# Pairwise attention pooling: transposes and Gram matrices once per four steps, Gram matrices through z's ring

## Chip, cores, metric

The kernel runs on one core of a Trainium2 chip. The metric is the time of one execution in microseconds, as the device measures it, median of several executions.

## What is computed

```python
B, F, D = x.shape                       # 2048, 39, 64; A = 64
row, col = np.triu_indices(F, k=1)      # 741 pairs of fields
ip = x[:, row, :] * x[:, col, :]
hidden = relu(einsum('bpd,da->bpa', ip, W_w) + b_w)
logits = einsum('bpa,a->bp', hidden, W_h) + b_h[0]
a = softmax(logits, axis=1)[:, :, None]
pooled = sum(a * ip, axis=1)
y = pooled @ W_p + b_p                  # [2048, 1], all f32
```

## The kernel before

Pooling and the last product are rearranged: y is the sum over pairs of a times the sum over d of x_i x_j W_p, and that inner sum is an entry of the Gram matrix of one batch, with one operand scaled by W_p. So each batch needs a 39x39 Gram matrix, and of the 741 pairs a hidden layer and a logit. The pairs are stored cyclically: field i with fields i+1 to i+19 (mod 39), so x lies widened to 58 columns (x_wide).

**Sizes.** Two batches share the 128 partitions (a "duo", 64 rows each). A step is 4 duos, 8 batches; there are 256 steps. Sixteen steps are a group, after which softmax and pooling run over 128 batches; 16 groups. Two steps are a "unit" (8 duos).

**One step.** VectorE multiplies 4 duos' pairs into prod (L265, 128x2964). TensorE puts them through the hidden layer in three chunks (hidden_layer, L438): a chunk is 8 matmuls in the code, 64 rows by 32 columns of the array each, 494 columns moved, into one of the two slots of z. ScalarE reads a slot with bias and relu into hidden (rectify, L349). When a step's three chunks are read, two half steps of logits follow on TensorE (first_half, second_half, L458, 8 matmuls each), which add to logits in PSUM. GpSimd places the head's weights for a later step (L226).

**One unit's cross work** (cross_work, L419) has three parts: 8 transposes of a later unit's x (L402), 16 matmuls for the Gram matrices of 8 duos (L413), both into the PSUM tile cross, and behind them VectorE's copies: x into x_wide in two pieces (spread, L250 and L251), the Gram matrices into gram_out (copy_gram, L272). ScalarE scales x by W_p (scale_x, L342), one instruction per unit. SyncE writes gram_out to DRAM, 8 DMAs per unit (L158, L160), and after the last unit of a group loads the values back in banded form, 8 DMAs (L172).

**z's ring.** Chunk n may be written when chunk n-2 has been read: TensorE waits at L432 for hidden_ready, which ScalarE counts up.

**Order.** Every engine's order is written out by hand; there is no scheduler. TensorE's is unit_work (L476). With "F" for a half step of logits and digits for the third of a hidden chunk, one unit is F 1 F 2 F 0 F 1 cross 2 0. Two units are the body of TensorE's inner loop (L518), four bodies a group, and the group loop (L514) holds the opening of logits (L448), which waits until ScalarE's exponentials (L357) have read the logits of the group before. VectorE, ScalarE and SyncE have loops of their own, of two, one and two groups.

```python
def body(k):
    unit_work(AHEAD * k, 0, 2 * k + 1, k + 3)
    unit_work(AHEAD * k + 2, 2, 2 * k + 2, k + 3)
...
with pe.Fori(0, GROUPS - 1) as g:
    pe.wait_ge(logits_free, g + 1)
    open_logits()
    with pe.Fori(0, GROUP_BLOCKS) as w:
        body(GROUP_BLOCKS * g + w)
```

Each f32 matmul of the code is two weight loads and two matmuls in the trace (so a chunk is 16 matmul records), a transpose one of each.

## Time and profile before

| | |
|---|---|
| median of 3 runs | 1133.52 us (1133.19 to 1134.34) |
| the profiled execution | 1133.69 us |
| its span in the trace | 1130.9 us |
| granted TensorE clock, mean over the span | 0.996 |
| TensorE matmuls (PE) busy | 1104.3 us, 98% |
| TensorE weight loads (PEld) busy | 515.5 us, 46% |
| VectorE (DVE) busy | 991.4 us, 88% |
| ScalarE (ACT) busy | 880.9 us, 78% |
| GpSimd (POOL) busy | 304.6 us, 27% |
| DMA | 45.80 MB, 40 GB/s |

The time of an execution holds 2.8 us that lie outside the span. A matmul's end in the trace is modelled and overlaps the next one's start, so start-to-start distances tell more than busy time. The chain of waits goes back from the last instruction, at each step to what released it, and so tells which engine sets the end.

### The profile page before, as it was taken

How to read it: one execution, taken by the hardware profiler on the slowest of the kernel's cores; microseconds unless marked ns; L12 is line 12 of the kernel's file. 1: busy time of each engine (PE TensorE's matmuls, PEld its weight loads, DVE VectorE, ACT ScalarE, POOL GpSimd, SP SyncE). 2: the span in 40 equal slices, each digit the busy share in tenths (PEclk: the TensorE clock that was granted, in tenths of full speed). 3: DMA queues.
4: the chain of work that ended last, by engine and by line, in shares of the span. 5: the costliest groups of instructions: out<-in, count | busy, mean ns of one | idle time of the engine just before them, and what ended most of it. 6: DMA issues, size and time to landing. Idle time of an engine off the chain costs nothing.

```text
span 1130.9 us, 61839 instructions
## 1 busy us (share of the span) xinstructions
PE 1104.3 (98%) x25856; PEld 515.5 (46%) x25856; DVE 991.4 (88%) x741; ACT 880.9 (78%) x929; POOL 304.6 (27%) x263
## 2 busy tenths in 40 slices
PE   6999999999999999999999999999999999999995
PEld 2444444444444444444444444444444444444442
DVE  7989989898898988989889898898989889898891
ACT  3878787787877778787777877877777787877884
POOL 2512214132141412314222141321414114141330
PEclk9999999999999999999999999999999999999998
DMA  2223242321323223132232313213222232321412
GB/s 43 39 43 43 36 47 39 43 40 34 51 38 46 39 36 47 34 52 38 35 50 37 46 34 45 44 34 49 39 37 44 40 46 37 52 36 34 48 25 23
DMA packets 341661, 45.80 MB, mean 40 GB/s; under 512 B 341600, under 2 KB 341600, under 8 KB 341600
## 3 DMA queue, kind: packets, MB, share of 16 engines
q1 hardware_dynamic: 340672, 45.20, 26.8%
q14 instruction: 49, 0.40, 0.2%
q8 instruction: 12, 0.20, 0.1%
q10 hardware_dynamic: 928, 0.00, 0.0%
HBM read 26.59 MB, written 18.54 MB: 40 GB/s over the span
## 4 chain that ended last, share of the span: by engine, by line
PE 95%; ACT 3%; issue 1%; SPq 0%; DVE 0%; DMA 0%; ACTq 0%; DVEq 0%
PE z L438 58%; PE logits L458 29%; PE cross L413 5%; PE cross L402 4%; ACT hidden L349 2%; ACT exps L357 1%; DMA x_rows<-in_r_x_dram 0%; SPq L178 0%; SPq L149 0%; DVE neg_max L278 0%; DVE weighted L287 0%; ACT x_scaled L342 0%; PE logits L448 0%; ACTq L348 0%; DVE x_wide L251 0%
## 5 line engine op out<-in xcount | busy, mean ns | idle before, releaser
L349 ACT ACTIVATE hidden<-z,b_col 128x988 f32<-128x988 f32 x768 | 819.0, 1084 | 224.1 <-PE z L438 223.6
L265 DVE TENSOR_TENSOR prod<-x_wide 128x2964 f32<-128x2964 f32 (+1 forms) x257 | 826.6, 3232 | 37.4 <-PE z L438 37.3
L438 PE MATMUL z<-prod,w_tiles 64*32 64x494 f32 x12288 | 790.4, 580 | 3.3 <-issue 2.2
L226 POOL COPY head_w<-head_cols 128x64 f32<-128x64 f32 x252 | 299.5, 1196 | 794.4 <-PE logits L458 794.4
L458 PE MATMUL logits<-hidden,head_w 64*32 64x371 f32 (+1 forms) x8192 | 437.1, 472 | 4.8 <-ACT hidden L349 3.2
L438 PEld LDWEIGHTS z<-prod,w_tiles 64*32 64x32 f32 x12288 | 236.9, 106 | 238.8 <-issue 117.6
L458 PEld LDWEIGHTS logits<-hidden,head_w 64*32 64x32 f32 x8192 | 180.6, 106 | 239.3 <-issue 234.3
L402 PEld LDWEIGHTS cross<-ident,x_rows 39*128 39x128 f32 x1024 | 42.2, 140 | 109.9 <-issue 109.9
L250 DVE COPY x_wide<-cross 128x312 f32<-128x312 f32 x128 | 61.4, 480 | 32.9 <-PE cross L413 30.4
L342 ACT ACTIVATE x_scaled<-x_wide,wp_col 128x312 f32<-128x312 f32 x128 | 70.2, 549 | 6.2 <-DVE x_wide L251 5.3
L413 PE MATMUL cross<-x_wide,x_scaled 64*39 64x39 f32 x4096 | 65.3, 204 | 0.0
L402 PE MATMUL cross<-ident,x_rows 39*128 39x39 f32 x1024 | 57.0, 236 | 7.2 <-DMA x_rows<-in_r_x_dram 7.2
L272 DVE COPY gram_out<-cross 103x312 f32<-103x312 f32 x128 | 60.4, 472 | 3.9 <-PE cross L413 3.9
L278 DVE TENSOR_REDUCE neg_max<-logits 128x1 f32<-128x742 f32 x16 | 14.9, 930 | 52.1 <-PE logits L458 52.1
L413 PEld LDWEIGHTS cross<-x_wide,x_scaled 64*39 64x39 f32 x4096 | 50.3, 114 | 7.5 <-issue 1.6
L251 DVE COPY x_wide<-cross 128x152 f32<-128x152 f32 x128 | 38.9, 304 | 0.0
L357 ACT ACTIVATE exps<-logits,exp_bias 128x742 f32<-128x742 f32 x16 | 14.0, 872 | 3.6 <-DVE exp_bias L281 3.6
L287 DVE CUSTOM_DVE_ANT_0 weighted<-exps,values 128x742 f32<-128x742 f32 x16 | 14.8, 923 | 1.0 <-ACT exps L357 1.0
L448 PEld LDWEIGHTS logits<-w_tiles 64*32 64x32 f32 x256 | 5.5, 105 | 7.9 <-issue 6.5
L293 DVE TENSOR_SCALAR y_all<-pooled,inv_sum,bp_col 128x1 f32 (+1 forms) x16 | 4.4, 274 | 3.0 <-DVE inv_sum L290 2.7
L342 ACT ACT_TABLE_LOAD x1 | 1.3, 1283 | 7.0 <-issue 7.0
L232 POOL COPY head_w<-head_cols 128x64 f32<-128x64 f32 x4 | 4.3, 1106 | 6.4 <-DMA head_cols<-in_L_rec_W_h_dram 6.4
(15 smaller groups left out, 18.2 us busy)
## 6 DMA issues: line engine op xcount, KB each, us to landing
x_rows<-in_r_x_dram SPq DMA_DIRECT2D x256, 78.0 KB
gram<-gram_out SPq DMA_DIRECT2D x512, 23.8 KB
gram<-gram_out SPq DMA_DIRECT2D x512, 11.6 KB
values<-gram SPq DMA_DIRECT2D x128, 46.3 KB, 3.4
out_dram<-y_all SPq DMA_DIRECT2D x8, 1.0 KB, 2.5
w_tiles<-in_L_rec_W_w_dram SPq DMA_DIRECT2D x4, 16.0 KB, 2.2
head_cols<-in_L_rec_W_h_dram ACTq DMA_DIRECT2D x4, 0.2 KB, 2.4
wp_col<-in_L_rec_W_p_dram ACTq DMA_DIRECT2D x2, 0.2 KB, 2.4
```

Source lines behind the costliest of these rows:

```text
L226: nc.gpsimd.tensor_copy(head_w[:, step % AHEAD, :, :], head_cols[:, :, at:at + TILE]).then_inc(head_w_ready, 1)
L250: nc.vector.tensor_copy(wide[:, :, :, 0:FIELDS], x_cols).then_inc(x_spread, 1)
L251: nc.vector.tensor_copy(wide[:, :, :, FIELDS:WIDE], x_cols[:, :, :, 0:OFFSETS]).then_inc(x_spread, 1)
L265: nc.vector.tensor_tensor(out, one, other, ALU.mult).then_inc(ready, 1)
L272: nc.vector.tensor_copy(gram_out[0:ROWS, slot, :, :, :], cross[0:ROWS, :, GCOLS].rearrange("p j (d f) -> p j d f", f=FIELDS)).then_inc(gra ...
L342: nc.scalar.mul(x_scaled[:, slot, :, :], x_wide[:, slot, :, 0:FIELDS], wp_col[:, 0:1]).then_inc(x_scaled_ready, 1)
L349: nc.scalar.activation(hidden[:, e, :, CHUNK * k:CHUNK * (k + 1)], z[:, (THIRDS * e + k) % 2, :, 0:CHUNK], ACT.Relu, bias=b_col[:, 0:1]).t ...
L357: nc.scalar.activation(exps[:, :, :], logits[:, :, 0:HCOLS], ACT.Exp, bias=exp_bias[:, 0:1], accum_out=exp_sum[:, :]).then_inc(logits_free, 1)
L402: last = nc.tensor.matmul(cross[:, j, FIELDS * q:FIELDS * (q + 1)], duo, ident[rows, :], is_transpose=True, start=True, stop=True, tile_po ...
L413: last = nc.tensor.matmul(cross[col:col + FIELDS, j, GCOLS.start + p * FIELDS:GCOLS.start + (p + 1) * FIELDS], x_scaled[row:row + D, slot, ...
L438: last = nc.tensor.matmul(z[col:col + TILE, (THIRDS * e + k) % 2, b, 0:CHUNK], w_tiles[row:row + D, col:col + TILE], prod[row:row + D, e, ...
L458: last = nc.tensor.matmul(logits[TILE * q:TILE * (q + 1), part, 0:cols], head_w[row:row + A, e, b, :], hidden[row:row + A, e, b, first:fir ...
```

## The change

A block of four steps takes the place of the unit wherever the unit was the grain:

- Cross work once per block: 16 transposes, then the Gram matrices of 16 duos (32 matmuls). Transposes go to x_cols, a PSUM tile of their own. Gram matrices go into a slot of z, as item 6 of a ring of now 13 items per block; ScalarE copies them out (copy_gram, L360 of the new kernel) and counts them in the same semaphore, now z_read.
- VectorE: no copies of Gram matrices; one pair of spreads per block, twice as wide.
- ScalarE: scale_x in four pieces per block, behind chunks 6, 7, 10 and, in the next block, 1; the copy behind chunk 5.
- TensorE's order: per block F 7 F 8 9 F 10 F 11 0 F 1 F 2 3 F 4 F 5 cross 6 (0 to 6 are of the next block). 13 is odd, so the slots swap from block to block; the loop body is now two blocks, run twice per group. The last group is written out without a loop.
- SyncE: half as many DMAs for x and for the Gram matrices, each twice as large.
- At the start the two halves of the first x arrive on semaphores of their own, and ScalarE spreads the second half. At the end half of the 8 stores of y are ScalarE's.

```diff
+    BLOCK_STEPS = 4
+    THIRDS = 3
+    CHUNKS = THIRDS * BLOCK_STEPS
+    ITEMS = CHUNKS + 1
+    CROSS_AT = CHUNKS // 2
+    def item(j):
+        return j + (j >= CROSS_AT)
...
+        def store_y(engine, h):
+            for q in range(QUADS):
...
-            load(0, 0)
+            sp.dma_start(x_rows[0:FIELDS, 0, :, :], x_rows_dram[0, :, 0, :, :]).then_inc(first_x_loaded[0], 16)
             for h in range(2):
                 for c in range(2):
                     sp.dma_start(w_tiles[...], w_hidden).then_inc(w_loaded, 16)
+            sp.dma_start(x_rows[D:D + FIELDS, 0, :, :], x_rows_dram[1, :, 0, :, :]).then_inc(first_x_loaded[1], 16)
             load(1, 1)
...
-                for m in range(GROUP_UNITS):
-                    unit = GROUP_UNITS * g + m
-                    if not (last and m >= GROUP_UNITS - 4):
-                        sp.wait_ge(cross_ready, unit + 3)
-                        load(unit + 4, m % SLOTS)
+                for m in range(GROUP_BLOCKS):
+                    v = GROUP_BLOCKS * g + m
+                    if not (last and m >= GROUP_BLOCKS - 2):
+                        sp.wait_ge(x_cols_ready, v + 2)
+                        load(v + 2, m % SLOTS)
...
+            def block_work(v, slot, pooled_group=None, ended=None, more=True):     # VectorE
+                multiply(v, slot, 0)
+                if pooled_group is not None:
+                    pool_group(*pooled_group)
+                for i in range(1, BLOCK_STEPS):
+                    multiply(v, slot, i)
+                if ended is not None:
+                    find_max(ended)
+                if more:
+                    spread(v + 1, 1 - slot)
...
+            def copy_gram(v, slot, writes):                                        # ScalarE
+                act.wait_ge(z_ready, ITEMS * v + CROSS_AT + 1)
+                if not (isinstance(writes, int) and writes == 0):
+                    act.wait_ge(gram_written[slot], 16 * GRAM_DMAS * writes)
+                nc.scalar.copy(gram_out[0:ROWS, slot, :, :, :],
+                               z[0:ROWS, (slot + CROSS_AT) % 2, :, 0:XCOLS].rearrange("p u (d f) -> p u d f", f=FIELDS)
+                               ).then_inc(z_read, 1)
...
+            def block_work(v, slot, writes, ended=None, more=True):
+                for j in range(CHUNKS):
+                    rectify(v, slot, j)
+                    if j == CROSS_AT - 1:
+                        if ended is not None:
+                            exponentials(ended)
+                        copy_gram(v, slot, writes)
+                    if j == 1 and not (isinstance(v, int) and v == 0):
+                        scale_x(v, slot, 3)
+                    if more and j in (6, 7, 10):
+                        scale_x(v + 1, 1 - slot, (6, 7, 10).index(j))
...
+            def gram_matrices(v, slot):                                            # TensorE
+                pe.wait_ge(x_scaled_ready, BLOCK_STEPS * (v + 1))
+                pe.wait_ge(z_read, ITEMS * v + CROSS_AT - 1)
...
+            def cross_work(v, slot, loads=None):
+                if loads is not None:
+                    pe.wait_ge(x_spread, 2 * (v + 1))
+                    pe.wait_ge(x_loaded[1 - slot], 32 * loads)
+                    transpose(1 - slot, range(2))
+                gram_matrices(v, slot)
...
-                    pe.wait_ge(hidden_ready, THIRDS * step + k - 1)
+                    pe.wait_ge(z_read, ITEMS * v + item(j) - 1)
...
+                first_half(v, 0)
+                chunks(7)
+                second_half(v, 0)
+                chunks(8, 9)
+                first_half(v, 1)
+                chunks(10)
+                second_half(v, 1)
+                chunks(11, 0)
...
+                chunks(5)
+                if following:
+                    cross_work(v + 1, 1 - slot, loads)
+                chunks(6)
+            def two_blocks(n):
+                block_work(2 * n, 0, n + 1)
+                block_work(2 * n + 1, 1, n + 2)
...
-                with pe.Fori(0, GROUP_BLOCKS) as w:
-                    body(GROUP_BLOCKS * g + w)
+                with pe.Fori(0, GROUP_BLOCKS // 2) as w:
+                    two_blocks(GROUP_BLOCKS // 2 * g + w)
...
-            with pe.Fori(BLOCKS - GROUP_BLOCKS, BLOCKS - 2) as k:
-                body(k)
+            two_blocks(BLOCKS // 2 - 2)
+            block_work(BLOCKS - 2, 0)
+            block_work(BLOCKS - 1, 1, following=False)
```

TensorE, the end of the first unit in the loop body of before: a hidden chunk (L438), the waits, the cross work, and the two chunks behind it. ISA and REGISTER_ALU are waits and their arithmetic; x8 counts matmuls as written.

```order
L421 ISA
L396 ISA
L402 MATMUL cross<-ident,x_rows 128x39 x8
L407 REGISTER_ALU
L413 MATMUL cross<-x_wide,x_scaled 39x39 x16
L432 REGISTER_ALU
L438 MATMUL z<-prod,w_tiles 32x494 x8
L430 REGISTER_ALU
L432 ISA
L438 MATMUL z<-prod,w_tiles 32x494 x8
```

The same place in the new kernel, the end of the second block of the loop body and the loop's way back (the two branches are the inner and the group loop's).

```order
L439 MATMUL x_cols<-ident,x_rows 128x39 x16
L444 REGISTER_ALU
L445 REGISTER_ALU
L452 MATMUL z<-x_wide,x_scaled 39x39 x32
L472 REGISTER_ALU
L474 REGISTER_ALU
L481 MATMUL z<-prod,w_tiles 32x494 x8
L567 REGISTER_ALU
L567 COMPARE_AND_BRANCH
L563 REGISTER_ALU
L563 COMPARE_AND_BRANCH
L491 MATMUL logits<-w_tiles 32x2 x8
```

Both counts doubled, the phase comes half as often, the Gram matrices wait for z's ring (L445), and one chunk instead of two stands behind them. The other pairs of adjacent chunks stand elsewhere; this is the one of chunks 8 and 9 (0 to 11 within a block) in the new order, ahead of a half step of logits (L501).

```order
L481 MATMUL z<-prod,w_tiles 32x494 x8
L472 REGISTER_ALU
L474 REGISTER_ALU
L481 MATMUL z<-prod,w_tiles 32x494 x8
L509 REGISTER_ALU
L510 REGISTER_ALU
L501 MATMUL logits<-hidden,head_w 32x370
```

Before there is one such pair per unit, two in four steps, and both stand behind cross work. Now there are three per block (8 9, 11 0, 2 3), none of them behind cross work.

ScalarE, one block of the new kernel (the third of the program); before, a unit was six of L349 and one x_scaled of 128x312.

```order
L356 ACTIVATE hidden<-z,b_col 128x2x494 x4
L365 COPY gram_out<-z 103x624
L356 ACTIVATE hidden<-z,b_col 128x2x494
L340 ACTIVATE x_scaled<-x_wide,wp_col 128x156
L356 ACTIVATE hidden<-z,b_col 128x2x494
L340 ACTIVATE x_scaled<-x_wide,wp_col 128x156
L356 ACTIVATE hidden<-z,b_col 128x2x494 x3
L340 ACTIVATE x_scaled<-x_wide,wp_col 128x156
```

The copy came from VectorE, and the scaling is cut in four.

## Rows read from the trace of the kernel before

**Rows 1.** Page: busy time by engine; the chain that ended last, by engine.
```profile
PE 1104.3 (98%) x25856; PEld 515.5 (46%) x25856; DVE 991.4 (88%) x741; ACT 880.9 (78%) x929; POOL 304.6 (27%) x263
...
PE 95%; ACT 3%; issue 1%; SPq 0%; DVE 0%; DMA 0%; ACTq 0%; DVEq 0%
```

**Rows 2.** Chain of waits, one unit from 521.84: start, us, what, records.
```profile
521.84 0.37 PE cross L402 x8
522.21 0.44 PE cross L413 x32
522.65 1.82 PE z L438 x32
524.47 0.62 PE logits L458 x16
525.09 0.95 PE z L438 x16
...
526.66 0.83 PE z L438 x16
...
530.39 0.37 PE cross L402 x8
```

**Rows 3.** Timeline of TensorE's weight loads, then matmuls, cross work at 530: start, us.
```profile
530.32 0.33 PEld L402 LDWEIGHTS cross<-ident,x_rows 39*128 39x128 f32 x8 [0.81 <-issue]
530.70 0.39 PEld L413 LDWEIGHTS cross<-x_wide,x_scaled 64*39 64x39 f32 x32
...
531.13 1.89 PE L438 MATMUL z<-prod,w_tiles 64*32 64x494 f32 x32
...
533.53 1.04 PE L438 MATMUL z<-prod,w_tiles 64*32 64x494 f32 x13
```

**Rows 4.** Windows: an ordinary unit, then one across a group's end.
```profile
521.77:530.32 8.55, 8.55 (x207) 3.99 (x200) 8.55 (x6) 6.76 (x7) 6.01 (x3) 1.00 0.23 39
...
504.17:513.22 9.05, 8.76 (x223) 4.38 (x217) 8.82 (x11) 7.52 (x9) 0.87 (x2) 1.00 0.22 38
```

**Rows 5.** Groups by line: busy us, mean ns, idle before, releaser.
```profile
L349 ACT ACTIVATE hidden<-z,b_col 128x988 f32<-128x988 f32 x768 | 819.0, 1084 | 224.1 <-PE z L438 223.6 <-issue 0.3
...
L342 ACT ACTIVATE x_scaled<-x_wide,wp_col 128x312 f32<-128x312 f32 x128 | 70.2, 549 | 6.2 <-DVE x_wide L251 5.3 <-DMA bp_col<-in_L_rec_b_p_dram 1.0
...
L272 DVE COPY gram_out<-cross 103x312 f32<-103x312 f32 x128 | 60.4, 472 | 3.9 <-PE cross L413 3.9
```

**Rows 6.** TensorE's timeline, start of the program.
```profile
14.12 3.55 PE L438 MATMUL z<-prod,w_tiles 64*32 64x494 f32 x32 [2.18 <-issue]
...
21.50 1.99 PE L438 MATMUL z<-prod,w_tiles 64*32 64x494 f32 x32 [1.08 <-ACT hidden L349]
...
24.78 0.55 PE L458 MATMUL logits<-hidden,head_w 64*32 64x371 f32 x8 [0.28 <-ACT hidden L349]
```

**Rows 7.** Timeline of SyncE's queue, end of the program.
```profile
1114.37 4.14 SPq L172 DMA_DIRECT2D values<-gram  x8
...
1123.30 3.76 SPq L208 DMA_DIRECT2D out_dram<-y_all  x8
```

**Rows 8.** DMA queues that carry instructions, in 0:45, 45:1055 and 1055:1131.
```profile
q8 instruction: 5, 0.08, 0.7%
...
q14 instruction: 47, 0.39, 0.2%
...
q8 instruction: 7, 0.11, 0.6%
```

**Rows 9.** Timeline of SyncE's queue: middle of its loop body, then its way back.
```profile
356.67 4.43 SPq L172 DMA_DIRECT2D values<-gram  x8
361.37 1.45 SPq L149 DMA_DIRECT2D x_rows<-in_r_x_dram  x2
...
425.70 4.51 SPq L172 DMA_DIRECT2D values<-gram  x8
434.54 0.85 SPq L149 DMA_DIRECT2D x_rows<-in_r_x_dram  x2
```

More of the change, by code:

```diff
@@ L299, in unit_work @@
                     find_max(ended)
-                multiply(2 * unit, unit, slot, 0)
-                if not (isinstance(unit, int) and unit + 1 >= UNITS):
-                    spread(unit + 1, 1 - slot)
-                copy_gram(unit - 1, 1 - slot, earlier)
-                if ended is not None:
-                    pool_group(ended, parity, loads)
-                multiply(2 * unit + 1, unit, slot, 1)
-            spread(0, 0)
-            multiply(0, 0, 0, 0, slice(0, QUADS, 2), first_prod_ready)
@@ new lines, in _ @@
+            spread(0, 0, first=True)
+            multiply(0, 0, 0, slice(0, QUADS, 2), first_prod_ready)
+            multiply(0, 0, 0, slice(1, QUADS, 2))
+            for i in range(1, BLOCK_STEPS):
+                multiply(0, 0, i)
+            spread(1, 1)
+            group(0)
+            with dve.Fori(0, (GROUPS - 2) // 2) as k:
+                group(2 * k + 1, (2 * k, 0, k + 1))
+                group(2 * k + 2, (2 * k + 1, 1, k + 1))
+            block_work(BLOCKS - 3, 1, pooled_group=(GROUPS - 2, 0, GROUPS // 2))
@@ L390, in _ @@
+            for m in range(GROUP_BLOCKS):
+                v = BLOCKS - GROUP_BLOCKS + m
+                block_work(v, m % SLOTS, v // 2, ended=GROUPS - 2 if m == 0 else None, more=m < GROUP_BLOCKS - 1)
             exponentials(GROUPS - 1)
+            act.wait_ge(y_ready, GROUPS)
+            store_y(act, 1)
         @block.tensor
         def _(pe):
-            def transpose(slot, loads):
-                pe.wait_ge(x_loaded[slot], 32 * loads)
-                nc.tensor.sem_inc(z_claimed, 1)
-                for q in range(QUADS):
-                    for j in range(2):
-                        rows = slice(j * D, j * D + FIELDS)
-                        duo = x_rows[rows, slot, 2 * q:2 * q + 2, :].rearrange("f h d -> f (h d)")
-                        last = nc.tensor.matmul(cross[:, j, FIELDS * q:FIELDS * (q + 1)], duo, ident[rows, :],
-                                                is_transpose=True, start=True, stop=True, tile_position=(j * D, 0))
-                return last
@@ L419, in cross_work, with transpose @@
-            def cross_work(m, slot, loads, with_x=True):
-                pe.wait_ge(gram_copied, m + 1)
-                if with_x:
-                    transpose(slot, loads)
-                gram_matrices(m + 1, slot).then_inc(cross_ready, 1)
-            def hidden_layer(step, e, k):
-                if isinstance(step, int) and step == 0:
+            def transpose(slot, tiles):
+                for d in range(ROW_DUOS):
+                    for u in tiles:
+                        rows = slice(u * D, u * D + FIELDS)
+                        duo = x_rows[rows, slot, 2 * d:2 * d + 2, :].rearrange("f h d -> f (h d)")
+                        last = nc.tensor.matmul(x_cols[:, u, FIELDS * d:FIELDS * (d + 1)], duo, ident[rows, :],
+                                                is_transpose=True, start=True, stop=True, tile_position=(u * D, 0))
+                last.then_inc(x_cols_ready, 1)
```

337 lines of the change are left out of this document (156 added, 181 removed).

## The prediction

> **What bounds the kernel now.** I read the page's busy times and chain first: the chain is TensorE for 95%, ScalarE for 3% [rows 1]. So time is won or lost where TensorE's order has something else than full chunks and logits. The chain over one unit [rows 2] shows this as a sum. A chunk is 0.83 us, a half step of logits 0.62, and a unit has six and four of them: 7.46 us. The unit takes 8.55 [rows 2, 4]. The other 1.09 us are 0.37 of transposes, 0.44 of Gram matrices, 0.16 in the two chunks behind them (1.82 in place of 1.66), and 0.12 in a chunk that takes 0.95. The last one is a wait on z's ring: the first chunk behind the cross work starts at 531.13, and the chunk that reuses its slot at 533.53 [rows 3], 2.40 us later, while two chunks and a half step (2.28) lie between. ScalarE idles 224 us waiting for z, and its relu takes 1084 ns [rows 5]: it is not full, it is the latency of the ring that counts. 128 such units are nearly the whole span; a unit across a group's end takes 0.50 more, 9.05 [rows 4].
>
> **The cross phase.** Per four steps before: 2 x (0.37 + 0.44 + 0.16) = 1.94 us. Afterwards there are 16 transposes and 64 matmul records of Gram matrices in one phase. What one more transpose or matmul costs is read from the weight loads [rows 3]: 8 loads of transposes fit in 0.33 us, of which the last one alone is about 0.14 (42.2 us over 1024 on the page), so three steps from pair to pair take 0.19, 0.06 each; 32 loads of Gram matrices fit in 0.39, the last about 0.11, so seven steps from four to four take 0.28, 0.04 each. The larger phase costs 0.37 + 4 x 0.06 = 0.61 and 0.44 + 8 x 0.04 = 0.76, and 0.16 at the edge once: 1.53. That saves 0.41 per block. Bounds: if nothing of the two phases is fixed except the edge, only 0.16 is saved; 0.45 if more of 0.37 is fixed.
>
> [...] The row shows 24 written matmuls in 0.81 us, 34 ns each [rows 2]. [...]
>
> **The ring.** The 2.40 us are the same for every pair of adjacent chunks. Before there are two pairs per four steps, 0.12 each, 0.24. Now there are three (8 9, 11 0, 2 3), and in each 2.28 us of work stand against 2.40. A chunk that starts late also loses what its second half restarts with, some 0.03. I take 0.14 each, 0.42, and 0.03 more between chunks 5 and 6, which have only the phase between them. That gives back 0.21 per block (bounds 0.12 and 0.30). The Gram matrices as a ring item do not wait: item 4's slot was read long before, and the copy of 103x624 must end before chunk 7, 0.76 + 0.83 + 0.62 us after the Gram matrices start. For its price the nearest rows are relu and scaling: 1084 ns for 988 elements, 549 for 312 [rows 5], so about 0.8 for 624. Chunk 7 needs the end of the Gram matrices (0.8), 0.1, 0.8 and 0.15 = 1.85, below 2.21. The copy costs nothing, with 0.3 us of cover.
>
> **ScalarE and VectorE.** ScalarE gets 64 copies (51 us), and its scalings go from 549 ns each to four of about 0.42 per block, 0.6 more per block. That makes 881 + 51 + 37 = 969 us, 87%. Scalings stand where the next chunk is a chunk plus a half step away (1.45 us): relu 0.98 in sequence and 0.33 fit. VectorE loses 60.4 us of Gram copies [rows 5] and some 20 us of spreads, down to some 910. The transposes now also wait for the spread of the block before, and logits for nothing new; the spread starts a phase's end after its transposes and lasts 1.3 us, a whole block before it is asked for. VectorE's four products (3.2 us each) follow the spread and are each needed at least 3 us after they end.
>
> **Group ends.** Before, the logits opened there wait for a relu that stands behind the exponentials. Now exponentials stand behind chunk 5, chunk 6 runs beside them, and the first half step needs no late relu: 0.50 becomes about 0.3. 15 ends, 3 us.
>
> **Start.** The first half step of logits starts at 24.78 [rows 6], with the same work done ahead of it before and now. Before, TensorE stands still 2.18 and 1.08 us there [rows 6] because ScalarE scales the second unit, which waits behind VectorE's products, before its first relu. That order is gone. I take 4 us; bounds 2 and 6.
>
> **End.** The 8 stores of y take 3.76 us to issue on one queue [rows 7], 1.9 on two. Against that the last values: the last Gram matrices come 9.5 us ahead of TensorE's end, in DMAs twice as large, and their 8 loads take 4.14 us to issue [rows 7]. Up to 2 us of wait are possible. I take 1 us of gain.
>
> **Sum.** 62 blocks of steady work x (0.41 - 0.21) = 12.4, group ends 3, start 4, end 1: 20.4 us. The span goes from 1130.9 to 1110.5. The profiled execution is 1133.69, 0.2 above the median of 1133.52; so 1133.7 - 20.4 = 1113. With the bounds (0.16 to 0.45, 0.12 to 0.30 per block) this case by itself is 1104 to 1124.
>
> **Rivals.**
>
> *TensorE's program falls out of its instruction memory at each group's way back.* This is the case on the other side, slower. Queue q8 brings TensorE's program in pieces of 16 KB: 5 pieces in the first 45 us, none between 45 and 1055 while the loops run, 7 when the last group is entered and left [rows 8]. By then the first lap was through about 440 + 850 entries, so a piece is about 256 entries, and at least six pieces are held at a time (the group loop lies in pieces 1 to 5, counted from 0, and the next is fetched ahead). Entries of the loop: 96 written f32 matmuls per unit with 4, 8 transposes with 2, are 400; the body of before is 800 and some 50 for waits. The new body is 1600 and some 90. It starts near entry 440, as before, and ends near 2170: pieces 1 to 8, and 9 is fetched ahead. It stays only if nine pieces fit. What a miss costs, SyncE's rows show: its loop body is left at the end of L172, 430.21, and goes on at 434.54, 4.3 us later, against 0.27 in the middle of the same body, 361.10 to 361.37 [rows 9], with instruction pieces on q14 [rows 8]. TensorE has a chunk queued then, 0.83, and the exponentials to wait for, so 3.0 to 4.1 us are lost per group, 14 times: 42 to 57 us. TensorE idle that long may also fall to the lower clock; two chunks take 3.55 us at the low level and 1.99 at the high one [rows 6], so up to 1.6 us or more each time. 1113 + 50 + 11 = 1174, range 1155 to 1200. If eight pieces or fewer are held, this decides. For it: SyncE's rows. Against it: no row shows TensorE's capacity, and its loops of before never miss.
>
> [...]
>
> *The phase saves only its edge.* If matmuls of 39 columns do not run closer in a long phase, the saving is 0.16 per block and the ring takes 0.21 back: 1133.7 + 3 - 8 = 1129, still faster by start and ends, and within 0.2% (2.3 us, about what a measurement of this kernel can tell from none) only if these fail too.
>
> *ScalarE becomes late.* If its copy from PSUM takes 1.2 us instead of 0.8 or the scalings 0.55, chunk 7 or 9 starts 0.1 to 0.3 late in each block: 1113 + 62 x 0.2 = 1125.
>
> **Chances.** Forecast, with ScalarE on time: 0.45, at 1113. ScalarE late 0.06, phase not dearer than its edge 0.05, both faster or the same. Instruction memory 0.42. Other slips 0.02. Faster by over 0.2% 0.54, within 0.03, slower 0.43. [...] The range must reach into the slower case: 1105 to 1190 holds nearly all of the faster cases and about two thirds of the slower one. The forecast's own range is 1104 to 1124.
>
> **What would show it.** Right: transposes of a block 16.85 to 16.95 us apart (17.10 now), 0.95 or so in one chunk of each of three pairs, cross phase 0.6 and 0.75, VectorE at 910 us, q8 silent between the first groups and the last. Wrong by the rival: q8 with pieces in every group, some hundred instead of 12, a hole of 3 to 4 us in TensorE every 68 us behind chunk 6, and a mean granted clock below 0.99. Wrong by ScalarE: waits of chunk 7 on gram_out L365.

## The result and the profile after

The changed kernel takes 1333.66 us (median of 4 runs, 1328.53 to 1338.32) against 1133.89 for the kernel before beside it: ratio 1.176, interval [1.172, 1.181]. That is slower by 200 us, on the other side of the forecast (1113) and beyond the range (1105 to 1190). The profiled execution took 1334.73 us, with a span of 1332.9.

The page of the changed kernel (busy times, granted clock over the span, instruction queues, the chain of waits by engine, groups of section 5):

```profile
PE 1156.1 (87%) x25856; PEld 517.9 (39%) x25856; DVE 934.6 (70%) x484; ACT 951.3 (71%) x1123; POOL 286.6 (22%) x263
...
PEclk9998989999899998989989899898998989989998
...
q8 instruction: 145, 2.38, 0.8%
...
q14 instruction: 11, 0.09, 0.0%
...
PE 85%; issue 12%; ACT 1%; DMA 1%; SPq 1%; ACTq 0%; DVE 0%; DVEq 0%
...
L491 PE MATMUL logits<-w_tiles 64*32 64x2 f32 x256 | 8.3, 185 | 96.3 <-issue 96.3
```

The number of matmuls is the same as before, the chain has 12% of "issue" in place of 1% [rows 1], and 96 us of idle time stand in front of the opening of the logits (L491), which happens 16 times. q8, which brings TensorE's program, moved 145 pieces in place of 12. It moved them all through the loops, 104 of them in the stretch 100:1045, where before there was none [rows 8]. The same stretch of the changed kernel, DMA queues:

```profile
q8 instruction: 104, 1.70, 0.8%
```

Where the time goes is read from TensorE's timeline over one way back of the group loop:

```profile
93.40 0.82 PE L452 MATMUL z<-x_wide,x_scaled 64*39 64x39 f32 x64
94.24 1.06 PE L481 MATMUL z<-prod,w_tiles 64*32 64x494 f32 x16
98.74 0.24 PE L491 MATMUL logits<-w_tiles 64*32 64x2 f32 x8 [3.44 <-issue]
102.57 0.28 PE L491 MATMUL logits<-w_tiles 64*32 64x2 f32 x8 [3.58 <-issue]
103.11 1.49 PE L501 MATMUL logits<-hidden,head_w 64*32 64x371 f32 x16 [0.26 <-issue]
104.32 1.93 PE L481 MATMUL z<-prod,w_tiles 64*32 64x494 f32 x16
...
109.41 1.06 PE L481 MATMUL z<-prod,w_tiles 64*32 64x494 f32 x16
...
120.30 0.56 PE L452 MATMUL z<-x_wide,x_scaled 64*39 64x39 f32 x34
122.18 0.50 PE L452 MATMUL z<-x_wide,x_scaled 64*39 64x39 f32 x30 [1.32 <-issue]
122.61 1.06 PE L481 MATMUL z<-prod,w_tiles 64*32 64x494 f32 x16
...
132.79 0.84 PE L501 MATMUL logits<-hidden,head_w 64*32 64x370 f32 x6
135.48 0.53 PE L501 MATMUL logits<-hidden,head_w 64*32 64x371 f32 x5 [1.86 <-issue]
...
137.39 0.47 PE L501 MATMUL logits<-hidden,head_w 64*32 64x370 f32 x1
```

Two holes stand next to each other, the second in the middle of sixteen equal little matmuls. No wait for data stands between them, so it is the program itself that is late: the branch back (L563) takes 3.85 us here, 3.4 to 4.0 at each of the 14 way backs, and q8 starts pieces at 95.6 and 99.9 us. The edge between two pieces lies there, eight matmuls into the opening; the trace has some 20 instructions of the loop ahead of it, so its first piece holds little more. Counted in the trace's instructions (a written f32 matmul is four), the two later holes lie 767 and 1279 behind this one, which is three and five pieces of 256. In e2_pad16 below, which puts 16 entries ahead of the loop, all three edges come 15 or 16 instructions earlier in the loop, and the pair of holes shows as one of 6.47 us ahead of the opening. Behind the first two holes a chunk ends 1.93 us after its start, in place of 1.06. The windows of the same group (length, busy us and count of PE, PEld, DVE, ACT, POOL, then granted clock, DMA share, GB/s), whole, its first lap, its second lap, and the stretch of the holes:

```profile
98.60:180.70 82.10, 71.52 (x1616) 32.22 (x1616) 58.54 (x31) 59.32 (x70) 18.24 (x16) 0.96 0.29 38
98.60:140.00 41.40, 34.24 (x708) 15.68 (x716) 24.37 (x13) 25.51 (x30) 5.08 (x7) 0.92 0.19 31
140.00:180.70 40.70, 37.28 (x920) 16.54 (x904) 34.17 (x18) 33.81 (x41) 13.16 (x9) 1.00 0.40 44
99.90:106.80 6.90, 3.98 (x56) 1.67 (x63) 2.80 (x1) 0.43 (x1) 0.00 (x0) 0.51 0.43 67
```

The granted clock is at its lower level, 0.51 over the last of these windows, for the 6.8 us from 100.0. TensorE had then been idle for 3.4 us, had done eight small matmuls and was in the second hole. A group takes 82.1 us. A group of the same code without holes takes 68.2 (shown below), so 13.9 are lost. From start to start: 3.64 in the first hole (chunk to opening 4.50 against 0.86), 3.76 in the second (opening to half step 4.37 against 0.61), 1.84 at the low clock (103.11 to 109.41 against 4.46), 1.54 in the first hole of the first lap (120.30 to 122.61 against 0.77), 2.19 in the second (half step to half step with two chunks between, 132.79 to 137.39, against 2.41). These are 13.0 of the 13.9. The second lap has no hole: its starts from transposes to transposes are 17.0 and 16.87 us.

### The profile page after: what moved, and what is told of

Read it like the earlier page. It is cut to its first block, busy times and chain, and to the rows that moved or that the text cites. A ratio compares the mean times of both kernels' runs of the same rounds, so it can differ in the third digit from the quotient of the medians.

```text
span 1332.9 us, 60251 instructions
## 1 busy us (share of the span) xinstructions
PE 1156.1 (87%) x25856; PEld 517.9 (39%) x25856; DVE 934.6 (70%) x484; ACT 951.3 (71%) x1123; POOL 286.6 (22%) x263
## 4 chain that ended last, share of the span: by engine, by line
PE 85%; issue 12%; ACT 1%; DMA 1%; SPq 1%; ACTq 0%; DVE 0%; DVEq 0%
PE z L481 52%; PE logits L501 25%; PE z L452 4%; PE x_cols L439 3%; ACT hidden L356 1%; PE logits L491 1%; DMA values<-gram 0%; DMA gram<-gram_out 0%; DMA bp_col<-in_L_rec_b_p_dram 0%; SPq L188 0%; ACTq L398 0%; SPq L176 0%; SPq L174 0%; ACTq L392 0%; ACTq L393 0%
## 5 line engine op out<-in xcount | busy, mean ns | idle before, releaser
L481 PE MATMUL z<-prod,w_tiles 64*32 64x494 f32 x12288 | 833.9, 590 | 4.6 <-ACT hidden L356 2.8
L501 PE MATMUL logits<-hidden,head_w 64*32 64x371 f32 (+1 forms) x8192 | 489.6, 491 | 33.9 <-issue 33.4
L501 PEld LDWEIGHTS logits<-hidden,head_w 64*32 64x32 f32 x8192 | 197.7, 109 | 279.3 <-issue 271.8
L259 DVE COPY x_wide<-x_cols 128x624 f32<-128x624 f32 (+1 forms) x64 | 51.4, 804 | 246.1 <-PE x_cols L439 244.1
L340 ACT ACTIVATE x_scaled<-x_wide,wp_col 128x156 f32<-128x156 f32 x256 | 105.9, 414 | 1.2 <-DMA bp_col<-in_L_rec_b_p_dram 1.2
L491 PE MATMUL logits<-w_tiles 64*32 64x2 f32 x256 | 8.3, 185 | 96.3 <-issue 96.3
L452 PE MATMUL z<-x_wide,x_scaled 64*39 64x39 f32 x4096 | 56.5, 202 | 20.6 <-issue 20.6
L365 ACT COPY gram_out<-z 103x624 f32<-103x624 f32 x64 | 43.4, 678 | 37.6 <-PE z L452 37.6
L439 PEld LDWEIGHTS x_cols<-ident,x_rows 39*128 39x128 f32 x1024 | 38.0, 139 | 57.5 <-issue 54.9
L452 PEld LDWEIGHTS z<-x_wide,x_scaled 64*39 64x39 f32 x4096 | 47.0, 113 | 26.3 <-issue 23.4
L439 PE MATMUL x_cols<-ident,x_rows 39*128 39x39 f32 x1024 | 45.6, 233 | 6.5 <-DMA x_rows<-in_r_x_dram 6.5
L491 PEld LDWEIGHTS logits<-w_tiles 64*32 64x32 f32 x256 | 6.2, 121 | 110.6 <-issue 110.6
L260 DVE COPY x_wide<-x_cols 128x304 f32<-128x304 f32 (+1 forms) x64 | 29.5, 461 | 0.0
```

The source lines that it names most:

```text
L259: nc.vector.tensor_copy(wide[:, :, :, 0:FIELDS], cols).then_inc(x_spread, 1)
L260: nc.vector.tensor_copy(wide[:, :, :, FIELDS:WIDE], cols[:, :, :, 0:OFFSETS]).then_inc(x_spread, 1)
L340: nc.scalar.mul(x_scaled[:, duos, :], x_wide[:, slot, duos, 0:FIELDS], wp_col[:, 0:1]).then_inc(x_scaled_ready, 1)
L365: nc.scalar.copy(gram_out[0:ROWS, slot, :, :, :], z[0:ROWS, (slot + CROSS_AT) % 2, :, 0:XCOLS].rearrange("p u (d f) -> p u d f", f=FIELDS) ...
L439: last = nc.tensor.matmul(x_cols[:, u, FIELDS * d:FIELDS * (d + 1)], duo, ident[rows, :], is_transpose=True, start=True, stop=True, tile_p ...
L452: last = nc.tensor.matmul(z[col:col + FIELDS, at, u, FIELDS * d:FIELDS * (d + 1)], x_scaled[row:row + D, duo, :], x_wide[row:row + D, slot ...
```

## The experiments

The table gives what the traces show of each: pieces on q8, start of the first opening of the logits, the first group, the mean of the 14 groups behind it, the time from the last opening to the end of TensorE's last matmul, and the time measured. e2, e3, e4 and e8 were executed once each; their differences are far larger than the spread of any kernel here.

| kernel | q8 | opening | group 1 | groups 2-15 | last | us |
|---|---|---|---|---|---|---|
| before | 12 | 24.2 | 68.9 | 68.9 | 61.5 | 1133.5 |
| changed | 145 | 19.2 | 79.5 | 82.1 | 70.4 | 1333.7 |
| e1_pad64 | 19 | 29.5 | 73.6 | 68.9 | 68.7 | 1151.1 |
| e2_pad16 | 145 | 21.5 | 84.1 | 82.1 | 68.5 | 1340.2 |
| e3_pad128 | 73 | 38.5 | 71.2 | 72.4 | 70.9 | 1211.2 |
| e4_before_two | 142 | 23.5 | 72.6 | 77.4 | 61.4 | 1254.2 |
| e5_fit | 19 | 19.3 | 74.3 | 69.2 | 70.3 | 1146.3 |
| e6_fit_load_first | 19 | 19.4 | 71.9 | 68.3 | 70.6 | 1134.0 |
| e7_slot | 19 | 21.2 | 73.2 | 68.3 | 67.2 | 1134.1 |
| e8_hint | 19 | 19.2 | 78.8 | 69.5 | 74.0 | 1161.4 |
| e9_short_tail | 12 | 21.0 | 73.7 | 68.5 | 65.6 | 1136.6 |
| e10_hint_load_first | 19 | 19.3 | 74.5 | 68.5 | 74.4 | 1143.1 |
| e11_slot48 | 19 | 21.8 | 69.0 | 68.3 | 67.5 | 1128.7 |
| e12_slot48_only | 20 | 21.1 | 71.1 | 68.5 | 67.4 | 1134.9 |

### Which pieces the loop lies in

**e1_pad64**, the changed kernel with this ahead of TensorE's group loop:

```
+            for _ in range(64):
+                nc.tensor.sem_inc(spare, 1)
             with pe.Fori(0, GROUPS - 1) as g:
```

> Edit: 64 semaphore increments that nobody waits for stand ahead of TensorE's group loop in the changed kernel; the loop and its work are untouched. They push the loop's first entry from about 477 to 541, so that it lies in pieces 2 to 8 of 256 entries instead of 1 to 8. Theory (eight pieces are held, the one fetched ahead included, so the loop must lie in seven): q8 falls silent between the first and the last group (some 15 pieces in all instead of 145), no hole at the way back, blocks 16.9 us apart throughout, granted clock 1.0, and the time is the 1113 us that was forecast for the other terms (1104 to 1124), plus at most 2 us for the 64 entries. Rival A (fewer than eight pieces are held, so seven pieces and one ahead do not fit either): 1300 to 1335 us, pieces in every group. Rival B (the hole at the way back is a wait of the new order, for example on logits_free behind the exponentials, and the pieces only follow it): nothing changes, 1333 us.

Measured 1151.12 us, ratio 1.015 [1.013, 1.018]. q8 brought 8 pieces up to 69 us, none until 1068, then 11. The page:

```profile
span 1150.6 us, 60315 instructions
...
q8 instruction: 19, 0.31, 0.1%
```

126 of the 145 pieces and 182 us go with 64 entries that do nothing. Rivals A and B fall: seven pieces and one ahead fit, and the order of the work is the same. But the time is 38 us above what the theory added to it, 1113; the sections below look for them.

**e2_pad16** is the same edit with 16 entries, **e3_pad128** with 128.

> Edit: 16 such entries instead of 64. The loop begins at about 493, still in piece 1, and ends in piece 8. Theory (pieces of 256 entries, eight held with the one ahead): nothing is gained, 1325 to 1340 us and about 145 pieces on q8, which shows that it is the edge between pieces that counts and not the entries or the later start. Rival A: also 1333. Rival B: 1333. Rival C (what counts is the size of the loop against some start offset, or the padding itself helps by delaying TensorE): a time between 1113 and 1333.

> Edit: 128 such entries. The loop begins at about 605 in piece 2 and ends at about 2336, in piece 9: again eight pieces and one ahead. Theory: slow again, 1300 to 1340 us, some 130 to 145 pieces on q8. Rival (only the number of the first piece matters, or a pad of any size above 35 helps): 1113 us as with 64.

e2_pad16 took 1340.18 us with 145 pieces, as expected: what counts is whether the loop's first entry lies behind the edge. e3_pad128 took 1211.18, with 73 pieces, between the two. Six of its way backs bring nine pieces, the others none; the two groups with none at either end take 68.3 and 68.6 us, the others 71.5 to 74.2. The loop reaches only some 40 entries into its eighth piece. The reading is that the piece behind it is asked for just before the branch and comes only at some way backs: q8 starts one at 178.2 us with the branch that starts at 178.1 and takes 4.60 us, and none at those that take 0.21. The theory gave the direction; its 1300 was wrong because it took that for certain.

**e4_before_two**, the kernel before with its body twice:

```
-                with pe.Fori(0, GROUP_BLOCKS) as w:
-                    body(GROUP_BLOCKS * g + w)
+                with pe.Fori(0, GROUP_BLOCKS // 2) as w:
+                    body(GROUP_BLOCKS * g + 2 * w)
+                    body(GROUP_BLOCKS * g + 2 * w + 1)
```

> Edit: the kernel before, with the body of TensorE's inner loop written out twice and half as many laps. Order, waits and work of every engine are as before; the loop is 1690 entries long, from about 480 to 2205. Theory: it becomes slow like the changed kernel, 1133 + 200 = 1333 us (1310 to 1350), with pieces in every group and the clock down once per group. Rival B (the new order causes the holes): 1133 us, q8 silent in the middle.

1254.15 us with 142 pieces. Nothing of the change is in it, and it loses 121 us. TensorE's timeline has the same pair of holes in the opening:

```profile
96.11 0.28 PE L448 MATMUL logits<-w_tiles 64*32 64x2 f32 x7 [3.31 <-issue]
98.97 0.29 PE L448 MATMUL logits<-w_tiles 64*32 64x2 f32 x9 [2.58 <-issue]
```

The size was missed by 80 us: 8.5 per group, not 14. The two later holes of the first lap are absent here. The first of them lies inside the Gram matrices, where two phases of the kernel before have become one and entries pass fastest. The other lies in an ordinary half step: its piece starts on q8 at 132.8 us, only as TensorE reaches its edge (the half step starts at 132.79), while the others behind the opening, in the lap of that timeline, start some 100 to 140 entries ahead of theirs. Why that one is fetched so late stays open.

### A hint in place of a shift

**e8_hint**, the changed kernel with

```
-            with pe.Fori(0, GROUPS - 1) as g:
+            with nc.Fori(0, GROUPS - 1, engines=[mybir.EngineType.PE], hint_back_edge=True) as g:
```

> Edit: the changed kernel as it was (loop in pieces 1 to 8, load of x behind the Gram writes), but each lap of the group loop begins with a hint that names its way back, so that the first piece can be fetched before the branch is taken. Theory (nine pieces for eight places: every piece of the loop has gone when it is wanted, and is fetched one ahead afterwards): the hint takes away the first hole of a group, 3.4 to 4.0 us, and perhaps the low clock behind it; the second hole and the nine pieces per group stay: 14 x 4 to 14 x 8 less than 1333, 1220 to 1280 us. Rival A (the hole at the way back is all that costs, since later pieces are fetched in time): about 1150, like the version that fits. Rival B (the hint finds no room, because the piece is pushed out again before the branch): 1333.

1161.38 us: near rival A, but for a reason that none of the three had. The loop stayed in pieces 1 to 8, and not one piece was fetched between 57 and 1071 us. The page:

```profile
q8 instruction: 19, 0.31, 0.1%
```

TensorE's timeline at the same way back:

```profile
97.03 1.06 PE L481 MATMUL z<-prod,w_tiles 64*32 64x494 f32 x16
98.03 0.44 PE L491 MATMUL logits<-w_tiles 64*32 64x2 f32 x16
98.76 0.86 PE L501 MATMUL logits<-hidden,head_w 64*32 64x371 f32 x16 [0.29 <-issue]
```

The opening follows the chunk after 1.00 us. The trace has an instruction BRANCH_PREFETCH_HINT at L563 in each of the 15 laps, 15 instructions more than the changed kernel in all, and the branch back takes 0.23 us, where the changed kernel's takes 3.83 (medians). That a piece is fetched on the hint is not shown: none came in the laps. Before the loops settle, q8 brings seven pieces here, the last at 56.7 us, and eight in e1_pad64, the last at 68.4. So eight pieces are held, and without the hint one of the eight places goes to the next piece in order, which the loop never needs. With it the loop may fill all eight. This and e1_pad64 settle the capacity: seven pieces and the one ahead fit (e1, e5 to e7), eight and the one ahead do not (changed, e2, e4), eight alone do (e8, e10).

### What was missing to the forecast

**e5_fit** puts the shift where TensorE has nothing to do:

```
             pe.wait_ge(ident_ready, 3)
+            for _ in range(12):
+                nc.tensor.matmul(x_cols[0:FIELDS, 1, BANK - 4:BANK - 2], ident[0:FIELDS, :], ident[0:FIELDS, 0:2],
+                                 start=True, stop=True, tile_position=(0, 0))
             pe.wait_ge(first_x_loaded[0], 16)
```

> Edit: the changed kernel with 12 small matmuls (48 entries, into columns of x_cols' bank that nobody reads) that TensorE does while it waits for the first x rows, in place of the 64 semaphore increments ahead of the loop. The group loop again begins in piece 2 (about entry 524) and ends in piece 8 (about 2256). Those 64 increments took TensorE from 19.5 to 29.5 us, 0.15 us each, and the clock fell behind them. Theory (it is only the piece of the first entry that counts): q8 silent from about 70 to 1060 us, the first opening of the logits at 19 to 21 us as in the changed kernel (29.5 with the increments), the first group 72 to 74 us, later groups 68.2 to 69.2 us as with the increments: 1138 to 1143 us. Rival (the 10 us hole came from the first lap's pieces, which come 5 to 9 us apart, and not from the increments): 1148 to 1152. The forecast's 1113 would need the 7 us in the last group, the 1 us per group in the middle and the first lap's 5 us to be gone too: not expected.

1146.31 us, 1.011 [1.010, 1.013]. The opening is at 19.3 as expected: the 64 increments had cost 10 us, about 0.14 us each (29.5 against 38.5 us with 64 more). Time and first group are above their ranges by some 3 us and a little.

**e6_fit_load_first** changes SyncE's order as well. What led to it are two views of e1_pad64. TensorE's chunk 11 is the first half of the first row, and ends by 487.4; ScalarE's relu of it is the last row, and starts 0.8 us later:

```profile
486.36 2.00 PE L482 MATMUL z<-prod,w_tiles 64*32 64x494 f32 x32
```

ScalarE, same stretch:

```profile
486.07 1.08 ACT L357 ACTIVATE hidden<-z,b_col 128x988 f32<-128x988 f32 x1 [0.33 <-PE z L482]
487.06 0.41 ACT L341 ACTIVATE x_scaled<-x_wide,wp_col 128x156 f32<-128x156 f32 x1
488.23 2.06 ACT L357 ACTIVATE hidden<-z,b_col 128x988 f32<-128x988 f32 x2 [0.76 <-PE z L482]
```

The view names z, but z was complete; x was being loaded at that time. The edit:

```
-                    if not (last and m >= GROUP_BLOCKS - 2):
-                        sp.wait_ge(x_cols_ready, v + 2)
-                        load(v + 2, m % SLOTS)
+                    if not (last and m >= GROUP_BLOCKS - 3):
+                        sp.wait_ge(x_cols_ready, v + 3)
+                        load(v + 3, (m + 1) % SLOTS)
```

with load(2, 0) behind a wait ahead of the first group.

> Edit: as e5_fit, and SyncE issues the load of x for block v + 3 as soon as the transposes of a phase are done, ahead of the eight writes of Gram matrices instead of behind them. In the run with 64 increments ScalarE's relu of chunk 11 began 0.2 to 0.8 us late in 21 blocks (7.9 us in all), with 389 to 699 packets of x in the 1.3 us before it; in the 15 blocks where no x load ran there it was never late. Theory (the traffic of the x load over that relu delays it): with the load 4 us earlier, relu 11 is no longer late; if the same traffic delays any relu, others (chunks 5 to 8) are late instead, with some of it hidden: between 0 and 9 us faster than e5_fit. Rival (the lateness belongs to chunk 11's place, behind the scaling of chunk 10, and the load has nothing to do with it): within 1 us of e5_fit and relu 11 late as often. A third: the x load now delays the Gram writes by 1.1 us, and the values at a group's end come later; VectorE would then show it at the pooling, and nothing on TensorE.

1134.03 us, 1.001 [1.000, 1.003], so 12 us less than e5_fit, more than the 9 expected. The late relus of chunks 10 and 11 fell from 10 to 12 us in all, by where lateness is counted from, to 1.2 to 1.5, and did not turn up elsewhere; 14 groups are 0.8 us shorter, and the first one 2.4. Why traffic at that place delays a relu, the traces do not say.

**e7_slot** drops the twelve matmuls and places the loop by its head:

```
+            with nc.Fori(0, GROUPS - 1, engines=[mybir.EngineType.PE], head_slot={mybir.EngineType.PE: 0}) as g:
```

> Edit: e6_fit_load_first without its 12 small matmuls; instead the group loop is told to begin at the first slot of a block of 256 entries, and TensorE jumps over the gap. [...] Theory (only the pieces in which the loop lies count, no matter how it got there): entry 512 to about 2244, pieces 2 to 8, q8 silent between 60 and 1045 us, groups 68.2 us, and 1131 to 1135 us, the same as e6_fit_load_first. Rival (the small matmuls at the start did something else, for example kept the clock up): a different first group or a different time by more than 3 us.

1134.14 us, 1.001 [1.000, 1.002]: as expected. The author counted slots in pieces of 256 entries, the distance that the edges of the changed kernel show (767 and 1279 instructions for three and five). The way over the gap is one branch: the trace has 60252 instructions, 60251 in the changed kernel, and the loop's line (L565) has a branch at 19.0 us that takes 1.92 us, where its way backs take 0.21. q8 brings eight pieces up to 59.4 us and none until 1053.6, so the loop lies in seven with one ahead. The small matmuls had not kept the clock up: from 12 to 100 us it is 1.00 here without them, and 1.00 and 0.98 in e6_fit_load_first and e5_fit, which have them. The groups are the same 68.3. The opening is 1.8 us later and the first group 1.3 longer, the last stretch is 3.4 shorter, so what runs once did change with the way the loop is placed.

**e9_short_tail** runs the last group's first two blocks in the loop:

```
+            with nc.Fori(0, GROUPS, engines=[mybir.EngineType.PE], head_slot={mybir.EngineType.PE: 0}) as g:
...
+                with pe.Fori(pairs * g, pairs * g + pairs - (g + 1) // GROUPS) as n:
+                    two_blocks(n)
```

> Edit: e7_slot, and the group loop also does the last group, with one lap of its inner loop in place of two (the end of the inner loop is worked out from the group's number), so that only the last two blocks are written out behind it, 1222 entries in place of 2899. Order and waits of the work stay. Theory (TensorE waits where code runs for the first time and 256 entries pass in less than the 4 to 5 us that a piece takes: in e6_fit_load_first holes of 0.6, 1.0, 1.4, 2.6, 0.8, 0.7, 1.1 and 0.6 us in the last 70 us): the holes of the last group's first two blocks go (0.4 + 0.8 + part of 1.4), some 13 pieces on q8 instead of 19, the rest stays: 2 to 4 us less than e7_slot, 1128 to 1132. Rival (the end is set by the last values' way over memory, which loads of the Gram matrices 1118 to 1122 us set): the time falls by as much as the last Gram matrices come earlier, since these are behind the same holes: also 2 to 3 us. Rival (holes come from the order in the last block, not from the code's first pass): no change, 1133.

1136.63 us, 1.003 [1.002, 1.004]: a miss. The last stretch fell by 1.6 us (67.2 to 65.6), but each group became 0.2 longer (68.3 to 68.5), 3 us in all. What is new in each group is the arithmetic of the inner loop's bounds; that it is the cause was not tested.

**e10_hint_load_first** is e8_hint with e6's order on SyncE, **e11_slot48** is e7_slot with 48 in place of 0, **e12_slot48_only** is the changed kernel with nothing but the head at slot 48.

> Edit: the changed kernel with both cures and no shift of the loop: the hint on the group loop's way back (as in e8_hint) and the load of x ahead of the Gram writes (as in e6_fit_load_first). In e8_hint the loop stayed in pieces 1 to 8, q8 brought 19 pieces in all and none between 57 and 1071 us, and the time was 1161. Theory (with the hint the piece fetched ahead at the loop's end is the one the branch goes to, not the tenth, so eight places hold the loop; and the load's traffic over relu 11 is a cost of its own of about 1 us per group): groups 68.2 us as in e6_fit_load_first in place of 69.4, first group and tail as the holes of the first pass have them: 1132 to 1140 us. Rival (the hint itself costs something in each lap, since e8_hint was 15 us slower than e5_fit with the same order of loads): groups of 69 us and 1145 to 1150.

> Edit: e7_slot with the group loop at slot 48 of its block in place of 0 (entry 560 to about 2292, still pieces 2 to 8). The work is the same. Theory (what is left of the loss sits where code runs for the first time, at the edges of pieces next to the cross phases, so it moves when the edges move by 48 entries): steady groups 68.2 us as in e7_slot, q8 19 pieces, but the first group (73.2 in e7_slot, 71.9 in e6_fit_load_first) and the last 67 to 70 us change by 1 to 3 us each, in either direction: 1130 to 1138. Rival (the first and the last group are slow for another reason, such as the start of the order or the last block's waits): first group and tail within 0.5 us of e7_slot.

> Edit: one line of the changed kernel: the group loop begins at slot 48 of a block of 256 entries. The load of x stays behind the Gram writes. Beside e11_slot48 (1128.7 us, groups of 68.2) only the order on SyncE differs. Theory (the x load's traffic over the relus of chunks 10 and 11 costs 0.7 to 0.9 us per group, as between e5_fit and e6_fit_load_first, groups of 69.1 against 68.3): groups of 68.9 to 69.2, first group and tail as in e11_slot48 or up to 2 us longer, 1138 to 1143 us. Rival (the 12 us between e5_fit and e6_fit_load_first were mostly the first group's holes, 74.3 against 71.9, and the tail's): 1130 to 1135.

e10_hint_load_first: 1143.14 us, 1.009 [1.006, 1.011], between both ranges. Its groups are 68.5, so the load's order gave its 1 us per group back and the hint costs 0.2; the last stretch is the longest of all, 74.4.

e11_slot48: 1128.70 us, ratio 0.9965 [0.995, 0.998], the fastest version, 0.35% faster than the kernel before. It is 1.3 us below the expected range. Work, order and groups are those of e7_slot. The first group went from 73.2 to 69.0, more than the 1 to 3 us of the theory and against the rival. The last stretch went from 67.2 to 67.5, which is the rival's "within 0.5 us". So moving edges are shown for the first group and not for the tail. The page:

```profile
PE 1093.0 (97%) x25856; PEld 484.4 (43%) x25856; DVE 932.7 (83%) x484; ACT 949.4 (84%) x1123; POOL 390.8 (35%) x263
...
PE 93%; ACT 2%; issue 2%; DMA 1%; SPq 1%; ACTq 0%; DVE 0%; DVEq 0%
```

e12_slot48_only: 1134.91 us (1129.18 to 1139.61 over 10 runs), 1.002 [1.000, 1.004], in the rival's range; its groups of 68.5 are below the theory's 68.9. One line of the program gives back 199 of the 200 us. The load's order is worth 6 us here, where it was 12 between e5 and e6; this profile has about 3 us of late relus, e5_fit's over 10.

## Why the prediction was wrong, and where it was right

**The choice: the step that failed.** The forecast took TensorE's loop to stay in its instruction memory, 0.45 against 0.42, and so put nothing into the sum for the way back. In the changed kernel the 14 groups in the middle are 13.1 us longer than before, 184 of the 202 us between the two spans. The first group adds 10.6, the last stretch 8.9 and what comes behind TensorE 3.6; the start gives 5.0 back. The reason for the choice was that "no row shows TensorE's capacity, and its loops of before never miss". That they never miss said nothing: they span five pieces, and would not miss with six places or with eight. What spoke for the miss was the count of entries, which was right (pieces 1 to 8, and 9 ahead), and a way back of SyncE that costs 4.3 us [rows 9]. The runs put TensorE's limit at eight pieces of 16 KB: seven and one ahead stay (q8: 19 pieces in e1_pad64), eight and one ahead do not (145). The rows of before show six held and the new loop wants nine; that step should have outweighed the silence of rows that could not have shown the limit. Nor were the loop's later edges free: three of them per group cost 3.76, 1.54 and 2.19 us.

**The rival's size.** Here too a step failed: "3.0 to 4.1 us are lost per group". One missing piece costs that, and the first hole has it: 3.64. But with nine pieces for eight places all nine come again (q8: nine per group), as if each piece that comes in pushed out the one wanted next. The loop's first piece holds only the loop's first few entries, so the second was wanted at once: 3.76 more. Two further ones came too late in the first lap, 1.54 and 2.19. The clock cost 1.84, where 0.8 was taken. At its low level a chunk takes 1.64 us from start to start (104.32 to 105.96) against 0.83; the row from which the prediction took the low level [rows 6] stands where the view shows a granted clock of 1.00. In all a group loses 13.9 us against one without holes, in place of 4 to 5.

**The cross phase and the ring: right.** A block without a hole, chain of waits of e11_slot48:

```profile
531.67 0.83 PE z L483 x16
532.50 0.62 PE x_cols L441 x16
533.12 0.75 PE z L454 x64
533.87 0.03 issue
533.89 1.06 PE z L483 x16
...
540.89 1.77 PE z L483 x32
...
549.40 0.62 PE x_cols L441 x16
```

Transposes take 0.62 (0.61 predicted), Gram matrices 0.75 (0.76), the edge 0.26 with the 0.03 of issue (0.16), and each of the three pairs 1.77 or 1.76, 0.10 above two chunks (0.14). The block is 16.90 or 16.87 us, inside 16.85 to 16.95, against 17.10. That it is met so closely is partly luck: the edge cost 0.10 more than forecast, the ring's pairs 0.1 less. 48 written matmuls in 1.37 us are 29 ns each, against 34 in the phase of before [rows 2]: the longer phase does run closer, as the forecast took from the row. ScalarE's copy takes 678 ns (0.8), a scaling 414 (0.42), and no chunk waits for it within a group.

**Group ends: wrong.** The forecast read the 0.50 of before as a late relu and took 0.2 off. Timeline of e11_slot48 at a group's end:

```profile
499.44 1.06 PE L483 MATMUL z<-prod,w_tiles 64*32 64x494 f32 x16
...
499.98 0.68 ACT L367 COPY gram_out<-z 103x624 f32<-103x624 f32 x1
...
500.30 0.27 PE L493 MATMUL logits<-w_tiles 64*32 64x2 f32 x16
...
500.91 0.86 PE L503 MATMUL logits<-hidden,head_w 64*32 64x371 f32 x16 [0.34 <-ACT gram_out L367]
```

The half step starts 0.61 us after the opening, which itself takes some 0.3. Before it was 0.59 (506.66 to 507.25). The view names ScalarE's copy as the releaser, but that ended at 500.66, 0.25 us before; what stands between is the opening, the entry into the inner loop and its registers. A group's end costs 0.66 now (68.2 less four blocks), so the term is a loss of 0.16 each, 2 us, in place of a gain of 3. With it a group is 68.2 where 67.9 was forecast: 4 us.

**Start: right in the changed kernel.** Its first opening is at 19.2 us, 5.0 earlier (4 predicted, 2 to 6); the first half step, which the prediction names, is at 21.33, 3.45 earlier, behind a hole of 1.33 in the opening. Placing the loop by its head leaves 2.4 of it, since the branch to the head, at 19.0 us, takes 2.50 us, where its way backs take 0.21 (L565); the first piece on q8 starts at 18.5. Start of e11_slot48:

```profile
18.84 1.06 PE L483 MATMUL z<-prod,w_tiles 64*32 64x494 f32 x16
21.79 0.27 PE L493 MATMUL logits<-w_tiles 64*32 64x2 f32 x16 [1.89 <-issue]
```

**End: wrong sign, within its warning.** The span ends 12.5 us behind TensorE in e11_slot48 and 11.4 before. The last values hold it up, the 2 us of wait that the prediction named as possible and did not take:

```profile
1109.63 4.22 SPq L188 DMA_DIRECT2D values<-gram  x8
...
1117.16 0.93 DVE L292 CUSTOM_DVE_ANT_0 weighted<-exps,values 128x742 f32<-128x742 f32 x1 [1.96 <-DMA values<-gram]
```

**What the forecast did not have: code that runs for the first time.** The last stretch is 67.5 us in e11_slot48 where before's was 61.5. Four blocks are written out there, some 2900 entries, and q8 brings 11 pieces; before, three units stood behind a loop there and 7 pieces came [rows 8]. TensorE waits where a piece is passed faster than the next one comes: a piece starts on q8 at 1102.1 inside the last Gram matrices of e7_slot:

```profile
1102.00 0.50 PE L454 MATMUL z<-x_wide,x_scaled 64*39 64x39 f32 x31
1104.47 0.51 PE L454 MATMUL z<-x_wide,x_scaled 64*39 64x39 f32 x33 [1.96 <-issue]
```

On q8 the pieces of that stretch start 4 to 9 us apart, and a block of 845 entries runs through 256 in 5.1 us on average, through those with a cross phase in less.

Against the forecast's span of 1110.5, e11_slot48 with 1126.4 lost 1.6 at the start, 1.1 and 0.6 in its first two groups and 4 in the others, 6.6 in the last stretch and 2.1 behind TensorE: 16.0 for the 15.9 that are to be explained. Apart from the group ends, the forecast was sound for the loop's steady part; it was short by some 10 us in what runs once. One of its bounds was too tight as well: with 0.16 saved and 0.30 given back per block its own sum gives 1134 and not 1124.

VectorE is busy 933 us, not 910: the 60.4 of Gram copies went [rows 5], and the 20 taken off for the spreads did not. It cost nothing.

## What to carry to other kernels

Before a loop's body is doubled, count its entries and where its first and last lie in blocks of 256. In these runs TensorE's loop nest stayed where it lay in seven such blocks (e1, e5 to e7, e11), or in eight with the hint on its way back (e8, e10). Where it was over by one, in the changed kernel, all nine were fetched again in each group, and the price was four holes and the lower clock, 13.9 us per group, not one hole; in e4 it was the two holes at the way back and the clock. Where a few dozen entries decide, place the loop's head and not the code ahead of it, and try two or three slots: between slot 0 and slot 48 lay 5 us, of which 4 in the first group, where the loop's code runs for the first time. When a profile shows "issue" in the middle of equal instructions, look at the instruction queue's pieces before looking at waits.

## What the runs showed of the hardware that was not expected

- With the hint on the way back (e8_hint) the next piece in order is not fetched in the laps that go back: q8 brings seven pieces ahead of them, not the eight of e1_pad64, and eight pieces stay for 1014 us.
- A semaphore increment that nobody waits for costs TensorE 0.14 us each (64 more of them: 9.0 us), while 12 matmuls of two columns at a time when it waited anyway cost nothing that shows (opening at 19.3 us in e5_fit, 19.2 in the changed kernel).
- Relus of chunks 10 and 11 started 0.2 to 1.8 us late while x was being loaded, in a random part of the blocks (in e1_pad64 in 20 of 42 with a load there, in none of 15 without). Started 4 us earlier, the same load delays almost none (e6 against e5). That edit also moves the Gram writes back behind the load; the 15 blocks have Gram writes too and no late relu. The mechanism is open.
- TensorE's granted clock fell to half (0.51 over 99.90:106.80) at the pair of holes at the way back (idle 3.44 and 3.58 us, eight small matmuls between), for 6.8 to 10.2 us, once in each group; the single holes in the first laps (idle 1.32 and 1.86 us) left it at 1.00 in all but one of the 14 groups in the middle. In e7_slot it fell for 3.4 us at 1105.0, behind the hole of 1.96 us shown above.
